# Folding with two stationary matrices, and no subtraction behind the fold

## The chip, the cores and the metric

One core of a Trainium2 chip runs the kernel. The metric is the device time of one execution in microseconds (us), the median of several runs. Below, PE is TensorE, DVE is VectorE, ACT is ScalarE, POOL is GpSimd and SP is SyncE.

## The reference

The input x has 64 batches of 32 rows and 512 columns. Two layers with residuals follow one another:

```python
def layer0(x, W0, condition):              # W0: (16, 32, 32)
    return x + jnp.einsum('bct,bcd->bdt', x, W0[condition])

def layer1(x, label, W, A, Bw):            # W: (512, 512), A: (5, 512, 32), Bw: (512, 32)
    base = jnp.einsum('bsi,oi->bso', x, W)
    low = jnp.einsum('bsi,bir->bsr', x, A[label])
    return x + base + 0.5 * jnp.einsum('bsr,or->bso', low, Bw)
```

The label of a batch is 0, 1 or 2 in the data; the kernel serves the labels 0 to 4.

## The kernel before

**Numbers.** PE multiplies operands of the rounded type float32r. Where a product needs more precision, a float32 value v is split into a rounded part `v_hi`, which ACT writes by a copy to float32r, and a remainder `v_lo`, which DVE writes as v minus `v_hi`. A product is then three matmuls: hi by hi, hi by lo, lo by hi.

**Order of the algebra.** The kernel applies layer 1 first, along the columns, and then layer 0, along the rows within a batch; both are linear. A tile is four batches, 128 rows by 512 columns; there are 16 tiles, worked on in 8 pairs (`pair`), of which pairs 1 to 6 are three turns of a loop with two pairs each (`Fori`). The order on each engine is written out by hand, and semaphores tie the engines together.

**Preparation.** PE transposes W (`transpose_w`, L522) after DVE has added the identity to its diagonal blocks (`add_identity`, L387). The term of label 0 is added to it as a product of two stacks (L556), so that `m_hi` and `m_lo` hold W transposed plus the identity plus what label 0 gives. DVE does all this in one long sequence, with the first two transposes of x in the middle of it. POOL builds `ident` and `fold_id`, a column of four 32 by 32 identities, and gathers the rows of W0 by indirect DMAs (L229), two for each pair.

**A pair.** DVE transposes x (L332), ACT and DVE split it into `xt_hi` and `xt_lo` (L259, L339). On PE:
- `low_pair` (L483 to L485) computes, for the four other labels, x times (A of that label minus A of label 0): 128 rows (label, r) by the 256 rows of the pair, in `p_low`.
- DVE multiplies by a 0/1 mask (`keep_low`, L352), so that each column keeps at most one of the four groups of 32 rows. ACT and DVE split the result: `kept_hi` (L295), `kept_lo` (L359).
- `fold_pair` (L501, L502) sums the four groups with the stationary matrix `fold_r`: four copies of `fold_id` side by side. So the sum stands four times in `p_fold`, in rows 0 to 31, 32 to 63 and so on. `kept_hi` goes through the matrix first, then `kept_lo` is accumulated onto it.
- ACT copies `p_fold` to `low_stack` in float32r (L303). DVE then overwrites the lower half, rows 64 to 127, with `p_fold` minus that rounded value (L444). So `low_stack` holds the rounded part twice, and then the remainder twice. `delta_tile` (L506) multiplies it by `b_stack`, and adds the product to `p_u`, which `main_tile` (L495 to L497) has filled with the product of x and m.
- `mix_tile` (L512 to L515) applies layer 0 to `u_hi` and `u_lo`, the parts of `p_u`, with a block-diagonal matrix `diag_hi` and `diag_lo`. DVE makes it from the gathered W0 (`mix` L448, `diag` L451). ACT copies the result to `y_sb` (L269), and SP stores it (L196).

**Order around the change.** On DVE the pair is: `keep_low`, first transpose, `kept_lo`, second transpose, `xt_lo` of the first tile of the next pair, then the subtraction L444, then `mix`, `diag`, `xt_lo` of the second tile, `diag_lo`, and the two `u_lo`. POOL's next gather waits for `diag` (L246). PE issues `delta_tile` as the last thing in a pair, after the wait for `s_stack` (L575). SP loads x two pairs ahead, but in one queue with the stores: the load of pair p + 3 stands behind the store of pair p (L196 to L202).

```python
            with sp.Fori(0, LOOPS) as g:
                for slot in range(2):
                    sp.wait_ge(s_xt, 2 * (2 * g + slot) + 2)
                    load(2 * g + slot + 2, slot)
                    store(2 * g + slot)
```

Of the kernel before, what the change touches and what calls it, by code (L numbers as in the profile page):

```python
# [27 lines left out]
F32 = mybir.dt.float32  # L28
F32R = mybir.dt.float32r
I32 = mybir.dt.int32  # L30
ALU = mybir.AluOpType
COPY = mybir.ActivationFunctionType.Copy

P = 128


def conditioned_lora_kernel(nc, x, cond, label, W0, W, A, Bw, out):
    B, S, T = x.shape
    NL, _, R = A.shape
    O = W.shape[0]  # L40
    BT = P // S
# [4 lines left out]
    Q = P // R  # L46
    ROWS = 2 * P
# [13 lines left out]
    with ExitStack() as ctx:  # L61
        def sb(name, shape, dt=F32):
            return ctx.enter_context(nc.sbuf_tensor(name, shape, dt))

        def ps(name, shape):
            return ctx.enter_context(nc.psum_tensor(name, shape, F32))

        def sem(name):
            return ctx.enter_context(nc.semaphore(name))
# [1 line left out]

        ident = sb("ident", [P, P])
        fold_id = sb("fold_id", [P, R])
        fold_r = sb("fold_r", [P, Q, R], F32R)
        block = sb("block", [P, BT])
        p_num = sb("p_num", [P, 1])
        group = sb("group", [P, 1])
# [36 lines left out]
        kept_hi = sb("kept_hi", [P, ROWS], F32R)  # L114
        kept_lo = sb("kept_lo", [P, ROWS], F32R)
        low_stack = sb("low_stack", [P, ROWS], F32R)
# [5 lines left out]
        p_fold = ps("p_fold", [P, O])  # L122
# [13 lines left out]
        s_group = sem("s_group")  # L136
# [21 lines left out]
        s_kepthi = sem("s_kepthi")  # L158
        s_keptlo = sem("s_keptlo")
        s_fold = sem("s_fold")  # L160
        s_foldhi = sem("s_foldhi")
        s_stack = sem("s_stack")


# [85 lines left out]
        @blk.scalar  # L250
        def _(act):
            act.dma_start(w_sb[:, 0], W[0:P, :]).then_inc(s_w_in[0], 16)

            act.dma_start(a_sb[:].rearrange("p l c r -> p l (c r)"), A_cols).then_inc(s_a_in, 16)

            def split_x(t, slot, u):

                act.wait_ge(s_xt, t + 1)
                nc.scalar.activation(xt_hi[:, slot, :, P * u:P * (u + 1)], xt[:, u], COPY).then_inc(s_xhi, 1)  # L259

            def split_u(n, u, bank, cols=slice(0, O)):

                act.wait_ge(s_u, n + 1)
                nc.scalar.activation(u_hi[:, u, cols], p_u[bank][:, cols], COPY).then_inc(s_uhi, 1)  # L264

            def copy_y(t, u):

                act.wait_ge(s_y, t + 1)
                nc.scalar.activation(y_sb[:, bass.ds(t, 1)], p_y[u][:].unsqueeze(1), COPY).then_inc(s_y_copied, 1)  # L269


            act.wait_ge(s_bT, 1)
            nc.scalar.activation(b_hi[:], p_y[0][:], COPY).then_inc(s_stack_hi, 1)
            act.wait_ge(s_adiff, 1)
            nc.scalar.activation(ad_hi[:], a_diff[:], COPY).then_inc(s_adhi, 1)
            act.wait_ge(s_aT, 1)
            nc.scalar.activation(a0_hi[:], p_y[1][:], COPY).then_inc(s_stack_hi, 1)
            split_x(0, 0, 0)
            act.wait_ge(s_less_hi, 1)
            nc.scalar.activation(b_stack[:], p_fold[:], COPY).then_inc(s_y_copied, 1)  # L280
            split_x(1, 0, 1)
            act.wait_ge(s_less_hi, 2)
            nc.scalar.activation(a0_stack[:], p_low[:], COPY).then_inc(s_y_copied, 1)

            def split_m(c):

                act.wait_ge(s_m, c + 1)
                nc.scalar.activation(m_hi[:, c], p_u[c][:], COPY).then_inc(s_uhi, 1)

            for c in range(C):  # L290
                split_m(c)

            def pair(p, slot, first=False, last=False):
                act.wait_ge(s_kept, p + 1)
                nc.scalar.activation(kept_hi[:], kept[:], COPY).then_inc(s_kepthi, 1)  # L295
                for u in range(2):
                    if not first:
                        copy_y(2 * p - 2 + u, u)
                    if not last:
                        split_x(2 * p + 2 + u, 1 - slot, u)  # L300
                    if u == 0:
                        act.wait_ge(s_fold, p + 1)
                        nc.scalar.activation(low_stack[:], p_fold[:, 0:ROWS], COPY).then_inc(s_foldhi, 1)  # L303
                act.wait_ge(s_diag32, p + 1)
                nc.scalar.activation(diag_hi[:, slot], diag[:, slot], COPY).then_inc(s_diaghi, 1)
                if not last:
                    split_u(2 * p, 0, 2 * slot)
                    split_u(2 * p + 1, 1, 2 * slot + 1)

            pair(0, 0, first=True)  # L310
            with act.Fori(0, LOOPS) as g:
                for slot in (1, 0):
                    pair(2 * g + 2 - slot, slot)
            pair(PAIRS - 1, 1, last=True)
            split_u(TILES - 2, 1, 3, left)
            split_u(TILES - 1, 0, 2)
            split_u(TILES, 1, 0, right)
            copy_y(TILES - 2, 0)

        @blk.vector  # L320
        def _(dve):
# [13 lines left out]
            def split_x(t, slot, u):  # L335

                dve.wait_ge(s_xhi, t + 1)
                cols = slice(P * u, P * (u + 1))
                nc.vector.tensor_tensor(xt_lo[:, slot, :, cols], xt[:, u], xt_hi[:, slot, :, cols].bitcast(F32),  # L339
                                        ALU.subtract).then_inc(s_xlo, 1)  # L340
# [22 lines left out]
            for j in range(BT):  # L363
                nc.vector.memset(group[R * j:R * (j + 1)], float(j)).then_inc(s_group, 1)
            nc.vector.memset(block[:], 0.0).then_inc(s_group, 1)
            dve.wait_ge(s_group, BT + 1)
            for j in range(BT):
                nc.vector.memset(block[R * j:R * (j + 1), j:j + 1], 1.0).then_inc(s_group, 1)
            dve.wait_ge(s_pool, 1)
# [14 lines left out]
            def add_identity(o):  # L384
                dve.wait_ge(s_w_in[o], 16)
                w_diag = w_sb[:, o, P * o:P * (o + 1)]
                nc.vector.tensor_tensor(w_diag, w_diag, ident[:], ALU.add).then_inc(s_diag, 1)  # L387
# [11 lines left out]
                nc.vector.tensor_scalar(to[:], ident[:], groups[:, 0:1], None, ALU.mult).then_inc(s_negative, 1)  # L399

            dve.wait_ge(s_pool, 4 + Q)
            add_identity(0)
            dve.wait_ge(s_x_in[0], 16 * Q)
            transpose_x(0, 0)
# [3 lines left out]
            split_x(0, 0, 0)  # L408
            add_identity(3)
            split_x(1, 0, 1)  # L410
            nc.vector.tensor_copy(fold_r[:], fold_id[:].unsqueeze(1).broadcast_to([P, Q, R])).then_inc(s_group, 1)
            dve.wait_ge(s_label_in, 16)
            nc.vector.tensor_scalar(keep[:], label_b[:], -1.0, group[:, 0:1], ALU.add,
                                    ALU.is_equal).then_inc(s_group, 1)
# [4 lines left out]
                nc.vector.tensor_tensor(m_lo[:, c], p_u[c][:], m_hi[:, c].bitcast(F32),  # L419
                                        ALU.subtract).then_inc(s_mlo, 1)  # L420

            dve.wait_ge(s_group, 2 * BT + 3)
            for c in range(C - 1):
                split_m(c)
            keep_low(0)
# [4 lines left out]
            def pair(p, slot, used, landed, first=False, last=False):  # L430
# [9 lines left out]
                if not last:  # L440
                    transpose_x(1 - slot, 1)
                    split_x(2 * p + 2, 1 - slot, 0)
                dve.wait_ge(s_foldhi, p + 1)
                nc.vector.tensor_tensor(low_stack[P // 2:P], p_fold[P // 2:P, 0:ROWS],  # L444
                                        low_stack[P // 2:P].bitcast(F32), ALU.subtract).then_inc(s_stack, 1)

                dve.wait_ge(s_w0_in[slot], 32 * used)
                nc.vector.tensor_tensor(mix[:, slot], w0_sel[:, bass.ds(2 * p, 2)],  # L448
                                        fold_id[:].unsqueeze(1).broadcast_to([P, 2, S]), ALU.add).then_inc(s_dve, 1)
# [27 lines left out]
        def _(pe):  # L477
            mm = nc.tensor.matmul
# [19 lines left out]

            def fold_pair():

                mm(p_fold[:, 0:ROWS], fold_r[:], kept_hi[:], start=True, stop=False)  # L501
                mm(p_fold[:, 0:ROWS], fold_r[:], kept_lo[:], start=False, stop=True).then_inc(s_fold, 1)  # L502

            def delta_tile(bank, u, cols=slice(0, O)):

# [112 lines left out]
```

## Time and profile before

| what | value |
|---|---|
| three runs | 94.54, 94.93, 95.05 us, median 94.93 us |
| span of the profiled execution, first to last instruction | 92.8 us |
| median less that span | 2.1 us |
| PE, DVE, ACT, POOL busy | 90%, 68%, 45%, 24% of the span |
| mean granted TensorE clock | 0.982 |
| HBM traffic | 5.96 MB read, 4.19 MB written |

The profiled execution is known by its span alone; what lies around the span in a timed run is taken as the 2.1 us between the two. A timeline row gives the start, the duration and the instruction, and in brackets how long the engine was idle before it and what ended that. The durations of successive instructions on an engine overlap, so the distance from start to start says what an instruction costs its engine. "PEld" is the weight load of PE, which runs beside the matmul before it. Clock 1.00 is 2.4 GHz, clock 0.50 is 1.2 GHz.

### The profile page before, as it was taken

The numbers are of one execution on the slowest core, as the hardware profiler recorded it, in microseconds if no ns is written. First come the engines' busy times: TensorE is split into PE (matmuls) and PEld (weight loads), VectorE is DVE, ScalarE is ACT, GpSimd is POOL, SyncE is SP. The second block draws the span as 40 slices with busy tenths as digits, with TensorE's granted clock in tenths as the row PEclk, the third lists the DMA queues.
The fourth block names the chain that finished last, engine by engine and source line by source line (L and its number), as shares of the span: only waits on it lengthen the run. The fifth ranks groups of instructions, "written<-read, shape, count | busy, mean of one in ns | idle before, by whom it ended". The sixth has DMA issues, their size and how long they took to land.

```text
span 92.8 us, 1445 instructions
## 1 busy us (share of the span) xinstructions
PE 83.6 (90%) x436; PEld 71.3 (77%) x436; DVE 63.1 (68%) x135; ACT 42.1 (45%) x82; POOL 22.1 (24%) x30
## 2 busy tenths in 40 slices
PE   2940979999999999999999999999999999999970
PEld 2930969988888898689878987898789868989950
DVE  2109997899988743994599549854986398624650
ACT  2321355625653643464346435543554355434540
POOL 5205779400620430026003500350044000000000
PEclk9999589999999999999999999999999999999999
DMA  1899985300000293019403920392048204100505
GB/s 14 242 204 214 277 153 161 92 0 0 10 15 0 99 262 106 0 73 286 107 0 119 275 72 0 136 264 67 0 164 242 61 0 161 69 7 0 226 0 226
DMA packets 13460, 10.21 MB, mean 110 GB/s; under 512 B 1808, under 2 KB 10896, under 8 KB 13456
## 3 DMA queue, kind: packets, MB, share of 16 engines
q1 hardware_dynamic: 12144, 9.31, 35.3%
q10 hardware_dynamic: 800, 0.59, 2.4%
q0 software_dynamic: 512, 0.26, 1.4%
q8 instruction: 2, 0.03, 0.2%
q14 instruction: 2, 0.02, 0.1%
HBM read 5.96 MB, written 4.19 MB: 110 GB/s over the span
## 4 chain that ended last, share of the span: by engine, by line
PE 68%; DMA 13%; SPq 5%; issue 5%; DVE 4%; ACT 1%; ACTq 0%
PE p_u L496 12%; PE p_u L495 12%; PE p_u L497 12%; DMA x_sb<-in_x 7%; DMA cond_b<-in_itok_B 6%; PE p_y L515 3%; PE p_y L512 3%; PE p_y L513 3%; PE p_low L483 3%; SPq L185 3%; PE p_low L485 3%; PE p_low L484 3%; PE p_u L506 3%; PE p_u L522 2%; PE p_fold L501 2%
## 5 line engine op out<-in xcount | busy, mean ns | idle before, releaser
L229 POOL DMA_INDIRECT w_sel<-in_L_cond_weights,w_row x16 | 17.8, 1112 | 42.2 <-DVE diag L451 39.2
L496 PE MATMUL p_u<-m_lo,xt_hi 128*128 128x512 f32 (+1 forms) x68 | 25.6, 377 | 0.0
L495 PE MATMUL p_u<-m_hi,xt_hi 128*128 128x512 f32 (+1 forms) x68 | 25.6, 377 | 0.0
L497 PE MATMUL p_u<-m_hi,xt_lo 128*128 128x512 f32 (+1 forms) x68 | 25.6, 377 | 0.0
L332 DVE STREAM_TRANSPOSE xt<-x_sb 128x512 f32<-128x512 f32 x16 | 17.3, 1091 | 6.7 <-DMA x_sb<-in_x 6.6
L345 DVE TENSOR_TENSOR u_lo<-p_u,u_hi 128x512 fp32r<-128x512 f32 (+1 forms) x17 | 10.6, 656 | 8.2 <-ACT u_hi L264 8.1
L259 ACT ACTIVATE xt_hi<-xt 128x512 fp32r<-128x512 f32 x16 | 10.1, 629 | 10.9 <-DVE xt L332 10.9
L495 PEld LDWEIGHTS p_u<-m_hi,xt_hi 128*128 128x128 f32 x68 | 12.8, 188 | 2.4
L497 PEld LDWEIGHTS p_u<-m_hi,xt_lo 128*128 128x128 f32 x68 | 12.8, 188 | 2.4
L496 PEld LDWEIGHTS p_u<-m_lo,xt_hi 128*128 128x128 f32 x68 | 12.8, 188 | 2.4
L264 ACT ACTIVATE u_hi<-p_u 128x512 fp32r<-128x512 f32 (+1 forms) x17 | 8.9, 571 | 7.7 <-PE p_u L506 7.7
L339 DVE TENSOR_TENSOR xt_lo<-xt,xt_hi 128x512 fp32r<-128x512 f32 x16 | 10.7, 669 | 0.4 <-ACT xt_hi L259 0.4
L269 ACT ACTIVATE y_sb<-p_y 128x512 f32 (+1 forms) x15 | 8.9, 591 | 3.0 <-PE p_y L515 3.0
L483 PE MATMUL p_low<-xt_hi,ad_hi 128*128 128x256 f32 x32 | 9.0, 282 | 0.0
L485 PE MATMUL p_low<-xt_hi,ad_lo 128*128 128x256 f32 x32 | 8.9, 279 | 0.0
L484 PE MATMUL p_low<-xt_lo,ad_hi 128*128 128x256 f32 x32 | 8.9, 279 | 0.0
L295 ACT ACTIVATE kept_hi<-kept 128x256 fp32r<-128x256 f32 x8 | 3.4, 420 | 9.5 <-DVE kept L352 8.1
L483 PEld LDWEIGHTS p_low<-xt_hi,ad_hi 128*128 128x128 f32 x32 | 6.0, 187 | 0.7 <-DVE xt_lo L339 0.4
L484 PEld LDWEIGHTS p_low<-xt_lo,ad_hi 128*128 128x128 f32 x32 | 6.0, 188 | 0.3
L512 PE MATMUL p_y<-u_hi,diag_hi 128*128 128x512 f32 (+1 forms) x16 | 6.2, 388 | 0.0
L513 PE MATMUL p_y<-u_hi,diag_lo 128*128 128x512 f32 (+1 forms) x16 | 6.2, 387 | 0.0
L515 PE MATMUL p_y<-u_lo,diag_hi 128*128 128x512 f32 (+1 forms) x16 | 6.1, 384 | 0.0
(77 smaller groups left out, 100.8 us busy)
## 6 DMA issues: line engine op xcount, KB each, us to landing
x_sb<-in_x SPq DMA_DIRECT2D x32, 128.0 KB
out<-y_sb SPq DMA_DIRECT2D x7, 512.0 KB
w_sb<-in_L_cond_W SPq DMA_DIRECT2D x3, 256.0 KB, 6.6
out<-y_sb SPq DMA_DIRECT2D x2, 256.0 KB
a_sb<-in_L_cond_lora_A ACTq DMA_DIRECT2D x1, 320.0 KB, 6.4
w_sb<-in_L_cond_W ACTq DMA_DIRECT2D x1, 256.0 KB, 3.2
w_sel<-in_L_cond_weights,w_row POOLq DMA_INDIRECT x16
bw_sb<-in_L_cond_lora_B_w SPq DMA_DIRECT2D x1, 64.0 KB, 3.4
```

Of the source, the lines that this page charges most:

```text
L229: nc.gpsimd.indirect_dma_start(out=w0_sel[:, t, :], out_offset=None, in_=W0_rows, in_offset=bass.IndirectOffsetOnAxis(ap=w0_row[:, t:t + 1 ...
L259: nc.scalar.activation(xt_hi[:, slot, :, P * u:P * (u + 1)], xt[:, u], COPY).then_inc(s_xhi, 1)
L332: nc.vector.transpose(xt[:, u].rearrange("p c (b s) -> p c b s", s=S), x_sb[:, slot, u].rearrange("p b (i c) -> p c b i", c=C)).then_inc(s ...
L339: nc.vector.tensor_tensor(xt_lo[:, slot, :, cols], xt[:, u], xt_hi[:, slot, :, cols].bitcast(F32), ALU.subtract).then_inc(s_xlo, 1)
L345: nc.vector.tensor_tensor(u_lo[:, u, cols], p_u[bank][:, cols], u_hi[:, u, cols].bitcast(F32), ALU.subtract).then_inc(s_ulo, 1)
L483: mm(p_low[:, 0:ROWS], ad_hi[:, c], xt_hi[:, slot, c], start=(c == 0), stop=False)
L484: mm(p_low[:, 0:ROWS], ad_hi[:, c], xt_lo[:, slot, c], start=False, stop=False)
L485: last = mm(p_low[:, 0:ROWS], ad_lo[:, c], xt_hi[:, slot, c], start=False, stop=(c == C - 1))
L495: mm(to, xt_hi[:, slot, c, rows], m_hi[:, c, cols], start=(c == 0), stop=False)
L496: mm(to, xt_hi[:, slot, c, rows], m_lo[:, c, cols], start=False, stop=False)
L497: mm(to, xt_lo[:, slot, c, rows], m_hi[:, c, cols], start=False, stop=False)
L512: mm(to[:, cols], diag_hi[:, slot, u], u_hi[:, u, cols], start=True, stop=False)
```

## The change

The fold gets two stationary matrices, kept in one tile `fold_to`. The first has `fold_id` in columns 0 to 63 (twice, 32 columns each) and zeros in columns 64 to 127; the second has zeros first and then `fold_id` twice. `kept_hi` goes through the first and `kept_lo` through the second, accumulated in the same bank. So `p_fold` holds the sum of `kept_hi` twice and then the sum of `kept_lo` twice, and ACT's copy (L303) writes the whole of `low_stack`. Its semaphore increment is now that of `s_stack`, for which PE waits. The subtraction L444, its wait and the semaphore `s_foldhi` are gone. For the new tile DVE clears `fold_parts` at its start, copies `fold_id` into two blocks of it before `add_identity(0)`, and casts all of it to `fold_to` where it made `fold_r`.

```diff
--- before.py
+++ after.py
@@ -71,7 +71,8 @@
 
         ident = sb("ident", [P, P])
         fold_id = sb("fold_id", [P, R])
-        fold_r = sb("fold_r", [P, Q, R], F32R)
+        fold_parts = sb("fold_parts", [P, 2, 2, 2, R])
+        fold_to = sb("fold_to", [P, 2, 2, 2, R], F32R)
         block = sb("block", [P, BT])
         p_num = sb("p_num", [P, 1])
         group = sb("group", [P, 1])
@@ -158,7 +159,6 @@
         s_kepthi = sem("s_kepthi")
         s_keptlo = sem("s_keptlo")
         s_fold = sem("s_fold")
-        s_foldhi = sem("s_foldhi")
         s_stack = sem("s_stack")
 
 
@@ -300,7 +300,7 @@
                         split_x(2 * p + 2 + u, 1 - slot, u)
                     if u == 0:
                         act.wait_ge(s_fold, p + 1)
-                        nc.scalar.activation(low_stack[:], p_fold[:, 0:ROWS], COPY).then_inc(s_foldhi, 1)
+                        nc.scalar.activation(low_stack[:], p_fold[:, 0:ROWS], COPY).then_inc(s_stack, 1)
                 act.wait_ge(s_diag32, p + 1)
                 nc.scalar.activation(diag_hi[:, slot], diag[:, slot], COPY).then_inc(s_diaghi, 1)
                 if not last:
@@ -363,7 +363,8 @@
             for j in range(BT):
                 nc.vector.memset(group[R * j:R * (j + 1)], float(j)).then_inc(s_group, 1)
             nc.vector.memset(block[:], 0.0).then_inc(s_group, 1)
-            dve.wait_ge(s_group, BT + 1)
+            nc.vector.memset(fold_parts[:], 0.0).then_inc(s_group, 1)
+            dve.wait_ge(s_group, BT + 2)
             for j in range(BT):
                 nc.vector.memset(block[R * j:R * (j + 1), j:j + 1], 1.0).then_inc(s_group, 1)
             dve.wait_ge(s_pool, 1)
@@ -399,6 +400,9 @@
                 nc.vector.tensor_scalar(to[:], ident[:], groups[:, 0:1], None, ALU.mult).then_inc(s_negative, 1)
 
             dve.wait_ge(s_pool, 4 + Q)
+            for part in range(2):
+                nc.vector.tensor_copy(fold_parts[:, part, part],
+                                      fold_id[:].unsqueeze(1).broadcast_to([P, 2, R])).then_inc(s_group, 1)
             add_identity(0)
             dve.wait_ge(s_x_in[0], 16 * Q)
             transpose_x(0, 0)
@@ -408,7 +412,8 @@
             split_x(0, 0, 0)
             add_identity(3)
             split_x(1, 0, 1)
-            nc.vector.tensor_copy(fold_r[:], fold_id[:].unsqueeze(1).broadcast_to([P, Q, R])).then_inc(s_group, 1)
+            dve.wait_ge(s_group, 2 * BT + 4)
+            nc.vector.tensor_copy(fold_to[:], fold_parts[:]).then_inc(s_group, 1)
             dve.wait_ge(s_label_in, 16)
             nc.vector.tensor_scalar(keep[:], label_b[:], -1.0, group[:, 0:1], ALU.add,
                                     ALU.is_equal).then_inc(s_group, 1)
@@ -419,7 +424,7 @@
                 nc.vector.tensor_tensor(m_lo[:, c], p_u[c][:], m_hi[:, c].bitcast(F32),
                                         ALU.subtract).then_inc(s_mlo, 1)
 
-            dve.wait_ge(s_group, 2 * BT + 3)
+            dve.wait_ge(s_group, 2 * BT + 6)
             for c in range(C - 1):
                 split_m(c)
             keep_low(0)
@@ -440,10 +445,6 @@
                 if not last:
                     transpose_x(1 - slot, 1)
                     split_x(2 * p + 2, 1 - slot, 0)
-                dve.wait_ge(s_foldhi, p + 1)
-                nc.vector.tensor_tensor(low_stack[P // 2:P], p_fold[P // 2:P, 0:ROWS],
-                                        low_stack[P // 2:P].bitcast(F32), ALU.subtract).then_inc(s_stack, 1)
-
                 dve.wait_ge(s_w0_in[slot], 32 * used)
                 nc.vector.tensor_tensor(mix[:, slot], w0_sel[:, bass.ds(2 * p, 2)],
                                         fold_id[:].unsqueeze(1).broadcast_to([P, 2, S]), ALU.add).then_inc(s_dve, 1)
@@ -498,8 +499,8 @@
 
             def fold_pair():
 
-                mm(p_fold[:, 0:ROWS], fold_r[:], kept_hi[:], start=True, stop=False)
-                mm(p_fold[:, 0:ROWS], fold_r[:], kept_lo[:], start=False, stop=True).then_inc(s_fold, 1)
+                mm(p_fold[:, 0:ROWS], fold_to[:, 0], kept_hi[:], start=True, stop=False)
+                mm(p_fold[:, 0:ROWS], fold_to[:, 1], kept_lo[:], start=False, stop=True).then_inc(s_fold, 1)
 
             def delta_tile(bank, u, cols=slice(0, O)):
```

DVE's order in the preparation, before (`w_sb<-w_sb,ident` is `add_identity`, `xt` are the transposes of x):

```order
L399 TENSOR_SCALAR b_negative<-ident,b_lo_groups 128x128
L399 TENSOR_SCALAR a_negative<-ident,a_lo_groups 128x128
L387 TENSOR_TENSOR w_sb<-w_sb,ident 128x128
L332 STREAM_TRANSPOSE xt<-x_sb 128x512 x2
L387 TENSOR_TENSOR w_sb<-w_sb,ident 128x128 x2
L339 TENSOR_TENSOR xt_lo<-xt,xt_hi 128x4x128
L387 TENSOR_TENSOR w_sb<-w_sb,ident 128x128
L339 TENSOR_TENSOR xt_lo<-xt,xt_hi 128x4x128
L411 CAST fold_r<-fold_id 128x128
```

and with the change, where the line numbers from L366 on have moved by one to five:

```order
L400 TENSOR_SCALAR b_negative<-ident,b_lo_groups 128x128
L400 TENSOR_SCALAR a_negative<-ident,a_lo_groups 128x128
L404 COPY fold_parts<-fold_id 128x64 x2
L388 TENSOR_TENSOR w_sb<-w_sb,ident 128x128
L332 STREAM_TRANSPOSE xt<-x_sb 128x512 x2
L388 TENSOR_TENSOR w_sb<-w_sb,ident 128x128 x2
L339 TENSOR_TENSOR xt_lo<-xt,xt_hi 128x4x128
L388 TENSOR_TENSOR w_sb<-w_sb,ident 128x128
L339 TENSOR_TENSOR xt_lo<-xt,xt_hi 128x4x128
L416 CAST fold_to<-fold_parts 128x256
```

Two copies stand now ahead of the first `add_identity`, and with it ahead of all that follows; the cast is 256 columns wide instead of 128. Neither list shows the clearing of `fold_parts`, which is near DVE's start.

DVE's order in the first pair of a loop turn, from `xt_lo` of the first tile of the next pair to its `diag_lo`, before (`mix` and `diag` are layer 0's matrices; ISA and REGISTER_ALU rows are register work and waits):

```order
L339 TENSOR_TENSOR xt_lo<-xt,xt_hi 128x4x128
L444 TENSOR_TENSOR low_stack<-p_fold,low_stack 64x256
L447 ISA
L448 ISA
L448 TENSOR_TENSOR mix<-w_sel,fold_id 128x64
L450 REGISTER_ALU
L451 TENSOR_TENSOR diag<-mix,block 128x256
L337 REGISTER_ALU
L339 TENSOR_TENSOR xt_lo<-xt,xt_hi 128x4x128
L457 TENSOR_TENSOR diag_lo<-diag,diag_hi 128x256
```

and with the change:

```order
L339 TENSOR_TENSOR xt_lo<-xt,xt_hi 128x4x128
L448 ISA
L449 ISA
L449 TENSOR_TENSOR mix<-w_sel,fold_id 128x64
L451 REGISTER_ALU
L452 TENSOR_TENSOR diag<-mix,block 128x256
L337 REGISTER_ALU
L339 TENSOR_TENSOR xt_lo<-xt,xt_hi 128x4x128
L458 TENSOR_TENSOR diag_lo<-diag,diag_hi 128x256
```

The subtraction is gone, and `mix` follows `xt_lo` directly. PE, ACT, POOL and SP issue the same instructions in the same order as before.

## Rows read from the trace of the kernel before

**Rows 1.** The page's part 4: the chain that ended last, shares of the span by engine
```profile
PE 68%; DMA 13%; SPq 5%; issue 5%; DVE 4%; ACT 1%; ACTq 0%
```

**Rows 2.** Stretch of one pair: us; busy PE, PEld, DVE, ACT, POOL; clock; DMA; GB/s
```profile
42.20:51.20 9.00, 9.00 (x47) 7.57 (x47) 6.63 (x12) 4.55 (x9) 2.09 (x3) 1.00 0.40 120
```

**Rows 3.** Waits of all engines: who waited for whom, us in total, times, longest
```profile
DVE xt L332 <- DMA x_sb<-in_x: 6.6, 5, 1.5
...
PEld p_fold L501 <- DVE kept_lo L359: 2.1, 5, 0.6
```

**Rows 4.** The chain of waits around 33 us: start us, us, what
```profile
33.41 3.36 DMA x_sb<-in_x
```

**Rows 5.** Timeline of DVE in the pair from 33 to 42 us, and into the next
```profile
39.82 0.43 DVE L444 TENSOR_TENSOR low_stack<-p_fold,low_stack 64x256 fp32r<-64x256 f32 x1
40.28 0.23 DVE L448 TENSOR_TENSOR mix<-w_sel,fold_id 128x64 f32<-128x64 f32 x1
...
40.88 0.69 DVE L339 TENSOR_TENSOR xt_lo<-xt,xt_hi 128x512 fp32r<-128x512 f32 x1
...
43.08 1.29 DVE L345 TENSOR_TENSOR u_lo<-p_u,u_hi 128x512 fp32r<-128x512 f32 x2 [1.18 <-ACT u_hi L264]
...
45.81 1.09 DVE L332 STREAM_TRANSPOSE xt<-x_sb 128x512 f32<-128x512 f32 x1 [1.10 <-DMA x_sb<-in_x]
```

**Rows 6.** Timeline of ACT in the same pair
```profile
38.78 0.39 ACT L303 ACTIVATE low_stack<-p_fold 128x256 fp32r<-128x256 f32 x1 [0.24 <-PE p_fold L502]
...
40.07 0.62 ACT L259 ACTIVATE xt_hi<-xt 128x512 fp32r<-128x512 f32 x1
```

**Rows 7.** Timeline of PE in the same pair: delta_tile
```profile
42.03 0.61 PE L506 MATMUL p_u<-b_stack,low_stack 128*128 128x512 f32 x2
```

**Rows 8.** Timelines of DVE and of PE in the last pair
```profile
84.76 0.43 DVE L444 TENSOR_TENSOR low_stack<-p_fold,low_stack 64x256 fp32r<-64x256 f32 x1 [2.53 <-ACT low_stack L303]
...
86.27 0.52 PE L506 MATMUL p_u<-b_stack,low_stack 128*128 128x256 f32 x2
```

**Rows 9.** The chain of waits from 9 to 18 us
```profile
13.14 0.60 issue
13.74 1.76 PE p_u L522 x12
```

**Rows 10.** Timeline of DVE in the preparation
```profile
4.23 0.43 DVE L373 TENSOR_SCALAR bw_rep<-bw_sb 128x512 f32<-128x512 f32 x1 [2.25 <-DMA bw_sb<-in_L_cond_lora_B_w]
...
9.69 1.40 DVE L399 TENSOR_SCALAR b_negative<-ident,b_lo_groups 128x128 fp32r<-128x128 f32 x1
11.00 0.28 DVE L399 TENSOR_SCALAR a_negative<-ident,a_lo_groups 128x128 fp32r<-128x128 f32 x1
11.20 0.30 DVE L387 TENSOR_TENSOR w_sb<-w_sb,ident 128x128 f32<-128x128 f32 x1
...
13.45 0.44 DVE L387 TENSOR_TENSOR w_sb<-w_sb,ident 128x128 f32<-128x128 f32 x2
...
15.22 0.21 DVE L411 CAST fold_r<-fold_id 128x128 fp32r<-128x128 f32 x1
15.36 0.24 DVE L413 TENSOR_SCALAR keep<-label_b,group 128x64 f32<-128x64 int32 x1
16.47 1.89 DVE L419 TENSOR_TENSOR m_lo<-p_u,m_hi 128x512 fp32r<-128x512 f32 x3 [0.87 <-ACT m_hi L288]
```

**Rows 11.** Timeline of POOL in the preparation
```profile
9.72 1.27 POOL L241 TENSOR_TENSOR ad_lo<-a_diff,ad_hi 128x512 fp32r<-128x512 f32 x1 [0.81 <-ACT ad_hi L275]
11.17 1.10 POOL L229 DMA_INDIRECT w_sel<-in_L_cond_weights,w_row  x1 [0.17 <-issue]
...
13.83 2.43 POOL L229 DMA_INDIRECT w_sel<-in_L_cond_weights,w_row  x1 [0.30 <-issue]
```

**Rows 12.** Two stretches of the preparation, columns as in rows 2
```profile
9.20:11.60 2.40, 2.35 (x11) 2.35 (x12) 2.12 (x11) 0.97 (x2) 1.70 (x2) 0.50 1.10 271
13.10:13.80 0.70, 0.10 (x2) 0.06 (x1) 0.70 (x3) 0.70 (x3) 0.42 (x1) 1.00 0.49 111
```

## The prediction

> **What bounds the kernel now.** I read the page's chain of waits first, then stretches of the pair loop, then the waits, and then timelines at the places that the diff touches. The chain shows PE in 68% of the span, DMA in 13%, and DVE in only 4% [rows 1]. In the stretch of one pair PE is busy for 9.00 of 9.00 us and DVE for 6.63 us [rows 2]. So in the pairs the matmuls set the pace, and DVE has some 2.4 us of slack in each. What else shows in the pairs is small: the weight load of the fold waits for `kept_lo` five times, 2.1 us in all [rows 3]. The reader should see why `kept_lo` is late. It stands behind a transpose, and that transpose waits for x from DMA, also five times, 6.6 us in all [rows 3]. The load takes 3.36 us in the chain [rows 4], and SP issues it behind a store. No row of waits names the subtraction L444 as something that PE waits for.
>
> **The subtraction goes.** It costs DVE 0.43 us, and `mix` starts 0.46 us after it [rows 5]; over eight pairs DVE loses 8 x 0.46 = 3.7 us of work. What is it worth to PE? In the pair shown it ends at 39.82 + 0.43 = 40.25, and `delta_tile`, which needs it, starts at 42.03 [rows 5, 7], so 1.8 us remain. ACT's copy, which now releases PE, ended at 38.78 + 0.39 = 39.17 [rows 6]; the margin grows to 2.9 us and PE gains nothing. The last pair is the tightest place: the subtraction ends at 84.76 + 0.43 = 85.19, and PE starts its `delta_tile` at 86.27 [rows 8], with 1.1 us in hand. Nothing there either. That ACT, not DVE, now gives `s_stack` adds no wait, since DVE had waited for the same copy.
>
> **What moves up behind it.** `mix` and `diag` start 0.46 us earlier. The `xt_lo` of the second tile would start at 40.42, but its input `xt_hi` ends at 40.07 + 0.62 = 40.69 [rows 6]; before it started at 40.88 [rows 5], so it gains at most 0.2 us. Then comes `u_lo`, before which DVE is idle for 1.18 us until ACT and PE have produced `u_hi` [rows 5]. The gain ends in that idle time, which grows to about 1.4 us. The next `kept` and the transposes stand behind `u_lo` and behind the load of x [rows 5], and neither comes earlier. POOL's gather starts 0.46 us earlier, because it waits for `diag`; nobody waits for the gathered rows. **Worth: 0 us.** The cover is the wait for `u_hi`. If it were gone, the upper end would be those 3.7 us, but PE with 9.00 us of 9.00 [rows 2] has no room to use them. PE can only win its 2.1 us of waiting [rows 3], and these hang on the load.
>
> **The fold itself.** Two matmuls of 128 x 256 stay two matmuls of 128 x 256, each with its own weight load as before. 0 us.
>
> **Clearing `fold_parts`.** 256 columns on DVE near 1.3 us. No row has a clear of this width. From below it is nothing, from above it is the 0.43 us of the 512-wide operation [rows 10]. Behind it DVE is idle for 2.25 us until `Bw` lands [rows 10]. 0 us, and still 0 us at the upper end.
>
> **The wider cast.** The cast of 128 columns delays its successor by 15.36 - 15.22 = 0.14 us [rows 10]. With 256 columns that may become at most twice as much, 0.28 us. Behind it DVE is idle for 0.87 us until ACT has `m_hi` [rows 10]. 0 us.
>
> **The two copies of 128 x 64.** They are the one addition without cover. From 9.69 us on DVE works without a stop, and the second `add_identity` (13.45 us) is what PE waits for: it ends near 13.45 + 0.27 = 13.72, and PE, after 0.60 us of standing, begins the transposes of W at 13.74 [rows 9, 10]. Whatever is put ahead of it moves PE, and from there on the chain is PE's own, or depends on PE through the store ahead of the load. Nothing later absorbs the shift. The price of a copy: the cast over 128 columns costs a step of 0.14 us. The operation over 512 columns takes 0.43 us against its 0.21 us, so 64 columns less save (0.43 - 0.21) / 384 x 64 = 0.04 us [rows 10]. That leaves 0.10 us each, **0.20 us together**. From below: half of the cast's step, 0.07 us each, so 0.14 us. From above: 0.24 us each, the full duration of the operation over 64 columns at 15.36 [rows 10], so 0.48 us. I take 0.20, since the cast is the nearest in kind.
>
> **Sum.** Against the profiled span: 92.8 + 0.2 = 93.0 us. The median of the runs lies 2.1 us above that span, and I leave this as it is: 94.93 + 0.20 = **95.13 us**. With the bounds, 95.07 to 95.41 us. About 0.5%, 0.47 us, is what a measurement of this kernel can tell from no change, so this forecast counts as within it.
>
> **Rival A: the earlier gather frees the load of x (faster).** In the pairs the load and the gather's transfers are under way together, and the first wait for x was longer than that of the next pair (up to 1.5 us, against 1.10 us [rows 3, 5]). If the gather's earlier start took transfers out of the load's way, all five waits could come down to 1.10 us: 6.6 - 5 x 1.10 = 1.1 us. The time would be 95.13 - 1.1 = 94.0 us. For it: PE does wait for this load, through `kept_lo`. Against it: the load lasts over 3 us [rows 4], and 0.46 us does not move the gather out of it. It decides if the load gets shorter than 3.0 us in each pair.
>
> **Rival B: the copies wait for POOL's gather (slower).** POOL starts the first gather at 11.17 us for 1.10 us [rows 11], and the copies would start at 11.20. The row of `b_negative` shows what such a meeting can cost: 1.40 us instead of 0.28 us, beside POOL's subtraction from 9.72 to 10.99 [rows 10, 11]. If the copies are held until the gather ends at 12.27, DVE and PE are late by 12.27 - 11.20 + 0.20 = 1.27 us, which gives 96.2 us. Against it: the cast at 15.22 and the operation at 15.36 ran inside a gather (13.83 to 16.26) and took 0.21 and 0.24 us [rows 10, 11]. That same gather was the longest, 2.43 us, so if one of the two loses it may be POOL, and its rows are used only by `mix` in the pairs. It decides if a copy lasts over 0.5 us.
>
> The Trainium skill speaks for this rival ("SBUF — State Buffer", "SBUF: two separate sides"): VectorE in a two-port mode, which a float32 copy enters, and GpSimd hold a shared port pair one at a time, and the one that starts later is blocked entirely. By it the sum would be Rival B's 1.27 us, not 0.20. The trace agrees for `b_negative` (1.40 us) and not for the cast at 15.22 us (0.21 us).
>
> **Rival C: PE's longer stop costs clock (slower).** After a long wait PE was granted 0.50 in the stretch 9.20 to 11.60; during the stop at 13.1 it kept 1.00 [rows 12]. The stop grows from 0.60 to 0.80 us. If it brought another such stretch, with half of 2.40 us lost: 95.13 + 1.2 = 96.3 us. Little speaks for it, as the clock did not stir at 0.60 us.
>
> **How the numbers follow.** Forecast 0.69, Rival A 0.12, Rival B 0.14, Rival C 0.05. Of the forecast's share 0.02 may fall below 94.46 and 0.02 above 95.40 by the scatter of runs (94.54 to 95.05). So faster by over 0.5% has 0.12 + 0.02 = 0.14, slower 0.14 + 0.05 + 0.02 = 0.21, and within 0.5% is left 0.65. The range takes in the forecast with its bounds and Rival B, and leaves out most of Rival A, and C: 94.3 to 96.2 us. The forecast's own range is 94.9 to 95.4 us.
>
> **What would show it.** In the new profile the two copies should take about 0.15 us each, the second `add_identity` start at 13.65 and PE's stop be about 0.8 us. DVE should be busy for some 3 us less, with `u_lo` idle for 1.4 us before it in the pairs, and PE's distance from pair to pair unchanged near 9.0 us. The forecast is wrong if a copy lasts over 0.5 us (B), if the waits for x fall clearly under 6.6 us (A), if the clock shows a second low stretch (C), or if PE waits for `s_stack` anywhere.

## The result and the profile after

| | before | changed |
|---|---|---|
| median of seven runs | 94.98 us | 97.36 us |
| lowest, highest | 94.54, 95.72 us | 96.32, 97.71 us |
| span of the profiled execution | 92.8 us | 94.5 us |

The ratio is 1.0246 with a 95% interval of [1.0202, 1.0290]: the change makes the kernel **slower by 2.4 us**. The prediction was 95.13 us, with a range that ended at 96.2 us. The ratios in this text leave disturbed runs out; where these are many (20 of the 31 runs of the kernel before in experiments 5 to 7, two of the four in experiment 3), a ratio lies up to 0.8% from that of the two medians beside it.

The profiled execution of the changed kernel is its fastest run, 96.32 us, so the two traces show 1.7 of the 2.4 us, and no trace shows the rest. First the page's busy times and its chain, by engine and by line:

```profile
PE 84.9 (90%) x436; PEld 72.0 (76%) x436; DVE 59.8 (63%) x130; ACT 41.4 (44%) x82; POOL 20.6 (22%) x30
...
PE 38%; DMA 24%; SPq 11%; DVE 10%; issue 10%; ACT 3%; ACTq 0%; DVEq 0%
DMA x_sb<-in_x 19%; SPq L185 7%; PE p_u L496 6%; PE p_u L498 6%; PE p_u L497 6%; DMA cond_b<-in_itok_B 5%; ACT y_sb L269 3%; SPq L196 3%; PE p_y L516 3%; PE p_y L513 3%; PE p_y L514 3%; DVE xt L332 3%; PE p_fold L502 2%; PE p_u L523 2%; DVE kept_lo L359 2%
```

In [rows 1] the chain lay on PE for 68% and on DMA for 13%. Now it is 38% and 24%, and the load of x leads the list by line. DVE is busy for 59.8 us instead of 63.1 us, so the removed work is gone as planned. It bought nothing.

The waits that answer to [rows 3] (us in total, times, longest; L502 is the fold's first matmul, L501 before):

```profile
DVE xt L332 <- DMA x_sb<-in_x: 8.8, 5, 2.1
...
PEld p_fold L502 <- DVE kept_lo L359: 4.4, 5, 1.2
...
PE p_fold L502 <- DVE kept_lo L359: 2.0, 3, 0.8
```

The transposes wait for x for 8.8 us instead of 6.6 us, again five times. The fold's weight load waits for `kept_lo` for 4.4 us instead of 2.1 us. The five loads as they stand in the chain of the changed kernel (start us, us, what):

```profile
32.95 3.83 DMA x_sb<-in_x
...
42.93 3.84 DMA x_sb<-in_x
...
52.84 3.19 DMA x_sb<-in_x
...
62.17 3.65 DMA x_sb<-in_x
...
71.88 3.28 DMA x_sb<-in_x
```

In the chain of the kernel before only two of the five appear, with 3.36 us [rows 4] and 3.26 us. Now all five are on it: PE waits in every one of these pairs. The stretch of one pair, with the columns of [rows 2], shows the hole in PE, 8.21 us busy of 9.00, where [rows 2] had 9.00 of 9.00:

```profile
42.80:51.80 9.00, 8.21 (x43) 6.70 (x42) 6.19 (x11) 4.07 (x9) 0.97 (x2) 1.00 0.33 84
```

**The same pair in both traces.** By chance SP begins to issue the load of one pair at 41.37 us in either trace. First POOL and SP of the kernel before:

```profile
41.24 1.15 POOL L229 DMA_INDIRECT w_sel<-in_L_cond_weights,w_row  x1 [7.85 <-DVE diag L451]
```

```profile
41.37 1.87 SPq L185 DMA_DIRECT2D x_sb<-in_x  x4
```

Then POOL and SP of the changed kernel:

```profile
40.63 0.95 POOL L229 DMA_INDIRECT w_sel<-in_L_cond_weights,w_row  x1 [8.26 <-DVE diag L452]
```

```profile
41.37 2.03 SPq L185 DMA_DIRECT2D x_sb<-in_x  x4
```

And DVE of the changed kernel, which answers to [rows 5]:

```profile
39.68 0.22 DVE L449 TENSOR_TENSOR mix<-w_sel,fold_id 128x64 f32<-128x64 f32 x1
39.94 0.42 DVE L452 TENSOR_TENSOR diag<-mix,block 128x256 f32<-128x256 f32 x1
40.73 0.69 DVE L339 TENSOR_TENSOR xt_lo<-xt,xt_hi 128x512 fp32r<-128x512 f32 x1 [0.37 <-ACT xt_hi L259]
...
43.07 1.29 DVE L345 TENSOR_TENSOR u_lo<-p_u,u_hi 128x512 fp32r<-128x512 f32 x2 [1.32 <-issue]
...
46.79 1.08 DVE L332 STREAM_TRANSPOSE xt<-x_sb 128x512 f32<-128x512 f32 x1 [2.10 <-DMA x_sb<-in_x]
```

The reader should see three things. `mix` follows `xt_lo` without the subtraction and starts at 39.68 (40.28 in [rows 5]). The gather starts at 40.63 instead of 41.24. And x, whose load was issued at the same time, releases the transpose at 46.79 instead of 45.81: **the load releases the transpose 0.98 us later, and of the transfers around it the gather is the one that moved ahead**. In the packet records of the two traces the load's last packet ends at 45.28 and at 45.94 us, so 0.66 us of the 0.98 lie in the packets. SP's four issues also take 0.16 us longer (2.03 against 1.87 us). That this isn't what makes the load late, experiment 4 shows: there two pairs with issues of 1.87 and 1.90 us wait for 1.72 and 1.97 us, where the kernel before, with issues of 1.87 and 1.89 us, waits for 1.10 and 1.22 us.

The sum over the pairs: when SP issues the store in front of the first load that PE waits for, the changed kernel is 0.44 us ahead (30.51 against 30.95 us), because data landed 0.81 us earlier in its preparation. The two chains show it, the kernel before first:

```profile
1.25 5.51 DMA cond_b<-in_itok_B
```

```profile
1.25 4.70 DMA cond_b<-in_itok_B
```

The five waits grow by 8.8 - 6.6 = 2.2 us. 92.8 - 0.44 + 2.2 = 94.6 us, and the span is 94.5 us. So the waits for x account for the whole difference of the two traces. The loop's pace says the same: the transposes that wait for x are (73.43 - 36.80) / 4 = 9.16 us apart before and (75.18 - 36.80) / 4 = 9.60 us after.

### The profile page after: what moved, and what is told of

Same layout as the page of the kernel before. It is cut to its first block, busy times and chain, and to the rows that moved or that the text cites. A ratio compares the mean times of both kernels' runs of the same rounds, so it can differ in the third digit from the quotient of the medians.

```text
span 94.5 us, 1439 instructions
## 1 busy us (share of the span) xinstructions
PE 84.9 (90%) x436; PEld 72.0 (76%) x436; DVE 59.8 (63%) x130; ACT 41.4 (44%) x82; POOL 20.6 (22%) x30
## 4 chain that ended last, share of the span: by engine, by line
PE 38%; DMA 24%; SPq 11%; DVE 10%; issue 10%; ACT 3%; ACTq 0%; DVEq 0%
DMA x_sb<-in_x 19%; SPq L185 7%; PE p_u L496 6%; PE p_u L498 6%; PE p_u L497 6%; DMA cond_b<-in_itok_B 5%; ACT y_sb L269 3%; SPq L196 3%; PE p_y L516 3%; PE p_y L513 3%; PE p_y L514 3%; DVE xt L332 3%; PE p_fold L502 2%; PE p_u L523 2%; DVE kept_lo L359 2%
## 5 line engine op out<-in xcount | busy, mean ns | idle before, releaser
L229 POOL DMA_INDIRECT w_sel<-in_L_cond_weights,w_row x16 | 16.2, 1013 | 45.5 <-DVE diag L452 42.6
```

The costliest lines, as they stand in the source:

```text
L229: nc.gpsimd.indirect_dma_start(out=w0_sel[:, t, :], out_offset=None, in_=W0_rows, in_offset=bass.IndirectOffsetOnAxis(ap=w0_row[:, t:t + 1 ...
```

## The experiments

**The theory (G).** Removing the subtraction brings `diag` forward, and with it POOL's gather. The gather's transfers now reach the DMA engines at the moment when the load of x begins there, and delay it. PE waits for that load, because it is issued late, behind a store. **Rivals.** The new preparation costs the time; the two matrices cost PE time; the new timing on DVE and ACT disturbs the pairs by itself.

**1. The preparation alone.** The kernel before, with `fold_parts` and `fold_to` made and never used:

```diff
+            nc.vector.memset(fold_parts[:], 0.0).then_inc(s_group, 1)
...
+            for part in range(2):
+                nc.vector.tensor_copy(fold_parts[:, part, part],
+                                      fold_id[:].unsqueeze(1).broadcast_to([P, 2, R])).then_inc(s_group, 1)
...
+            dve.wait_ge(s_group, 2 * BT + 4)
+            nc.vector.tensor_copy(fold_to[:], fold_parts[:]).then_inc(s_group, 1)
```

> The kernel before, with only the preparation of the change added: fold_parts is cleared, filled by the two copies and cast to fold_to, and nothing uses it (fold_r is still made and used). Theory G (the earlier gather delays the load of x): no change in the pairs, so 95.0 to 95.3 us, the waits of the transposes for x near 6.6 us. Rival P (the preparation costs the time, by the copies or by where it leaves the engines): near 97.3 us.

Measured: 94.35 us against 94.41 us of the kernel before on that chip, ratio 0.9994 [0.9920, 1.0069]. The five waits for x in its trace are 6.5 us. The preparation isn't the cause. Its own 0.2 us is below what this comparison can tell.

**2. The removal alone.** The matrix stays, the subtraction goes; the lower half of `low_stack` is then not the remainder:

```diff
-                dve.wait_ge(s_foldhi, p + 1)
-                nc.vector.tensor_tensor(low_stack[P // 2:P], p_fold[P // 2:P, 0:ROWS],
-                                        low_stack[P // 2:P].bitcast(F32), ALU.subtract).then_inc(s_stack, 1)
```

> The kernel before, with only the subtraction behind the fold left out (the lower half of low_stack then holds the rounded part instead of the remainder) and the one matrix fold_r kept. Theory G: DVE comes to diag 0.46 us earlier and POOL's gather with it, so the load of x is late as in the changed kernel: 97.0 to 97.5 us, waits for x near 8.8 us. Rival P, and a rival by which the two matrices themselves cost time on PE: 94.9 to 95.1 us.

Measured: 95.88 us against 94.41 us, ratio 1.0175 [1.0094, 1.0255]. Its wait for x:

```profile
DVE xt L332 <- DMA x_sb<-in_x: 8.5, 5, 2.2
```

Leaving work out makes the kernel slower, with 8.5 us of waiting, and without the new matrices. The size is under the 97.0 us expected; the kernel before ran 0.6 us faster on this chip than in the first comparison, which is part of that.

**3. The gather alone, first try.** The kernel before whole; only POOL's wait is another:

```diff
-                    pool.wait_ge(s_diag32, p - 1)
+                    pool.wait_ge(s_dve, p)
```

> The kernel before whole, with one edit on POOL: the gather for a pair waits for mix of two pairs earlier instead of for diag, and so starts some 0.5 us earlier. DVE, ACT and PE do the same work. Theory G: 96.8 to 97.6 us, waits for x near 8.8 us. A rival by which DVE's or ACT's new timing itself delays the pairs: 95.0 us.

Measured: 95.69 us against 94.41 us, ratio 1.0064 [0.9949, 1.0178]. Not enough to tell, and under the forecast. The trace is of its run of 96.01 us, above its median, and shows waits for x of 7.3 us, between the two kernels. In the table below this run's gather does not come as early, measured against the load, as that of the changed kernel.

**4. The gather alone, second try.** The kernel before with the gather released by the end of the subtraction, some 0.25 us earlier again. So that the semaphore of the gathered rows stays in order, DVE's wait for them stands now ahead of the subtraction:

```diff
-                    pool.wait_ge(s_diag32, p - 1)
+                    pool.wait_ge(s_stack, p - 1)
...
+                dve.wait_ge(s_w0_in[slot], 32 * used)
                 dve.wait_ge(s_foldhi, p + 1)
...
-                dve.wait_ge(s_w0_in[slot], 32 * used)
```

> The kernel before, with the gather waiting for the end of the subtraction instead of for diag, some 0.7 us earlier than in the kernel before and 0.2 to 0.3 us earlier than in the run in which it waited for mix (DVE's wait for the gathered rows stands ahead of the subtraction now, where it costs nothing). Theory G: the first gather ends within 0.2 us after SP begins to issue the load of x in every second pair, as in the changed kernel, so waits for x of 8 to 9.5 us and 96.3 to 97.5 us, with all of DVE's, ACT's and PE's work as before. A rival by which the gather alone cannot do it: under 95.7 us.

Measured: 96.82 us against 94.81 us, ratio **1.0217 [1.0177, 1.0257]**. All the work of the kernel before, in the same order on every engine, and nearly the whole loss of the change (1.0246). Waits, and in one pair POOL's gather beside SP's load:

```profile
DVE xt L332 <- DMA x_sb<-in_x: 8.3, 5, 2.0
...
PEld p_fold L501 <- DVE kept_lo L359: 3.9, 5, 1.1
```

```profile
59.34 0.95 POOL L229 DMA_INDIRECT w_sel<-in_L_cond_weights,w_row  x1 [7.40 <-DVE low_stack L445]
```

```profile
60.17 1.90 SPq L185 DMA_DIRECT2D x_sb<-in_x  x4
```

No row of waits shows DVE waiting for the gathered rows, so the moved wait costs nothing. This settles where the time comes from.

**5. The subtraction's time put back.** The changed kernel, with a subtraction of the same size on DVE that writes a tile nobody reads:

```diff
+                dve.wait_ge(s_stack, p + 1)
+                nc.vector.tensor_tensor(spare[P // 2:P], p_fold[P // 2:P, 0:ROWS],
+                                        low_stack[P // 2:P].bitcast(F32), ALU.subtract).then_inc(s_spare, 1)
```

> The changed kernel, with a subtraction of the same size put back on DVE at the old place; it writes a spare tile that nobody reads. PE, the matrices and the values are those of the changed kernel. Theory G: diag and with it the gather move back by 0.46 us, and the time returns to that of the kernel before plus the 0.2 us of the preparation: 94.3 to 95.2 us, waits for x near 6.6 us. A rival by which the matrices cost time on PE: 2 us over the kernel before.

Measured: 94.79 us against 95.12 us, ratio 1.0029 [0.9965, 1.0092]. The waits for x are 6.8 us. Useless work on DVE brings the loss back to nothing. The matrices are cleared too.

**6. The gather later.** In the changed kernel, and then in the kernel before, the gather waits for `diag_lo`:

```diff
-                    pool.wait_ge(s_diag32, p - 1)
+                    pool.wait_ge(s_diaglo, p - 1)
```

> The changed kernel, with one edit on POOL: the gather waits for diag_lo instead of diag, and so starts some 1.3 us later than in the changed kernel, 0.7 us later than in the kernel before. Theory G: its transfers fall in the middle of the load of x or behind it, and the time comes back to 94.5 to 95.3 us, waits for x at or under 6.6 us. The rivals leave it at 97.3 us.

> The kernel before, with the gather waiting for diag_lo instead of diag, some 1.3 us later. Theory G: like the changed kernel with the same edit, 92.3 to 93.2 us on this theory alone, waits for x near 5.6 us.

Measured: the changed kernel 92.72 us against 94.41 us, ratio 0.9838 [0.9756, 0.9919]; the kernel before 94.12 us against 95.12 us, ratio 0.9961 [0.9899, 1.0024]. The wait for x of the changed kernel with this edit:

```profile
DVE xt L332 <- DMA x_sb<-in_x: 5.6, 5, 1.3
```

The waits came out as expected in both, 5.6 and 5.2 us. Both times missed. The changed kernel became faster than both kernels, 1.8 us under the 94.5 to 95.3 us expected, so the direction held and the size did not; the kernel before on that chip was 0.6 us faster than in the first comparison. The kernel before with the edit came out 0.9 us over its 92.3 to 93.2 us.

**7. The gather behind the whole load.** Again in both kernels:

```diff
-                    pool.wait_ge(s_diag32, p - 1)
+                    pool.wait_ge(s_kept, p)
```

> The changed kernel, with the gather for a pair waiting for kept of the pair before (instead of diag of two pairs before), some 4 us later than in the changed kernel: its transfers fall behind the whole load of x. Theory G: the load of x runs alone, waits of the transposes for x at or under the 5.6 us of the run with the gather behind diag_lo, time 92.2 to 93.0 us. If that other run won by something else than the distance to the load: 93.5 us or more.

> The kernel before, with the same edit on POOL. Theory G: the subtraction is worth nothing once the gather is out of the load's way, so the same time as the changed kernel with this edit, less the 0.2 us of its preparation: 92.0 to 92.9 us. If the subtraction's removal has a cost or a gain of its own in the pairs, the two differ by over 0.5 us.

Measured: the changed kernel 93.51 us against 95.12 us, ratio 0.9908 [0.9853, 0.9962]; the kernel before 94.06 us against 95.12 us, ratio 0.9954 [0.9903, 1.0005]. The wait for x in the changed kernel with this edit, and one such transpose:

```profile
DVE xt L332 <- DMA x_sb<-in_x: 4.9, 5, 1.0
...
PEld p_fold L502 <- issue: 0.2, 1, 0.2
```

```profile
44.70 1.09 DVE L332 STREAM_TRANSPOSE xt<-x_sb 128x512 f32<-128x512 f32 x1 [0.96 <-DMA x_sb<-in_x]
```

The waits are 4.9 us, and 4.7 us in the kernel before with this edit, the shortest of all. The weight load of the fold waits for 0.2 us, and no longer for `kept_lo`. So the pairs run at PE's own pace, (71.56 - 35.84) / 4 = 8.93 us. Both medians lie above the forecasts, by 0.5 and 1.2 us. The traces were of the fastest runs (92.73 and 92.54 us), and can't show what made the others slower; that stays open. The two ratios overlap, so whether the removal is worth anything once the gather is away stays open here.

**The dose.** For the last four pairs with a wait for x, from the traces: how long after SP begins to issue the load (SP L185) POOL ends the first of its two gathers (L229, start plus duration), and how long the transposes then wait in these four pairs together.

| kernel | first gather ends after the load's issue begins, us | waits for x, four pairs, us |
|---|---|---|
| before, gather with the subtraction (4) | 0.1 to 0.4 | 6.99 |
| changed | 0.2 to 0.5 | 6.84 |
| before, subtraction left out (2) | 0.2 to 0.5 | 7.34 |
| before, gather behind `mix` (3) | 0.4 to 0.7 | 5.47 |
| before | 1.0 to 1.3 | 5.03 |
| before, with the preparation (1) | 1.0 to 1.3 | 4.90 |
| changed, with the useless subtraction (5) | 1.0 to 1.3 | 5.13 |
| changed, gather behind `diag_lo` (6) | 1.6 to 1.9 | 4.36 |
| before, gather behind `diag_lo` (6) | 1.7 to 2.0 | 4.14 |
| changed, gather behind `kept` (7) | 4.5 to 4.8 | 3.83 |
| before, gather behind `kept` (7) | 4.5 to 4.8 | 3.76 |

The later the gather, the shorter the waits, up to the scatter: two kernels with the same distances differ by up to 0.5 us in the sum, and single pairs by some 0.3 us. The largest step lies between a gather that ends 0.2 to 0.5 us after and one that ends 0.4 to 0.7 us after. Kernels with and without the subtraction lie on one curve. The kernel before stood on its slope: with 5.03 us against 3.76 us it paid for the gather too, only less. The first of the five pairs isn't counted here: in some of these kernels its first gather ends before the load's issue begins, and its wait doesn't follow the order of the table (1.34 us with the gather with the subtraction, 1.53 us before, 1.98 us changed).

**8. The load of x ahead of the store.** If the gather hurts only because PE waits for the load, an earlier load must make it harmless:

```diff
+            sp.wait_ge(s_xt, 2)
+            load(2, 0)
-            with sp.Fori(0, LOOPS) as g:
+            with sp.Fori(0, LOOPS - 1) as g:
                 for slot in range(2):
-                    sp.wait_ge(s_xt, 2 * (2 * g + slot) + 2)
-                    load(2 * g + slot + 2, slot)
+                    sp.wait_ge(s_xt, 2 * (2 * g + slot) + 4)
+                    load(2 * g + slot + 3, 1 - slot)
                     store(2 * g + slot)
+            sp.wait_ge(s_xt, 2 * (PAIRS - 4) + 4)
+            load(PAIRS - 1, 1)
+            store(PAIRS - 4)
+            store(PAIRS - 3)
```

> The changed kernel, with one edit on SP: the load of x for pair p + 3 is issued ahead of the store of pair p, not behind it; the gather still waits for diag. Theory G says that the early gather costs time only because PE waits for the load of x that stands behind the store. With the load ahead it has several us in hand: waits of the transposes for x near 0 in the pairs, none of kept_lo, PE near 8.9 us a pair as in the run with the gather behind kept, so 92.5 to 93.9 us although the gather is as early as in the changed kernel. If the early gather disturbs something else too: 95 us or more.

> The kernel before, with the same edit on SP. Theory G: the same pace in the pairs, and without the 0.2 us of the new preparation: 92.3 to 93.9 us, within 0.5 us of the changed kernel with this edit. If the removed subtraction is worth something once the load is out of the way, the changed kernel with this edit is faster by over 0.5 us.

> The changed kernel, with both edits: the load ahead of the store, and the gather behind diag_lo. Theory G: no gain over the load ahead of the store alone, as neither is waited for then: within 0.4 us of it.

Measured, against 94.97 us of the kernel before: changed 93.68 us, ratio 0.9877 [0.9818, 0.9936]; before 93.56 us, ratio 0.9865 [0.9799, 0.9931]; changed with the late gather 92.76 us, ratio 0.9793 [0.9710, 0.9876]. Two stretches of the first, columns as in [rows 2], and one of its transposes:

```profile
36.00:45.00 9.00, 9.00 (x48) 7.72 (x47) 6.23 (x12) 4.49 (x10) 1.89 (x2) 1.00 0.39 121
45.00:54.00 9.00, 9.00 (x48) 7.72 (x47) 6.23 (x12) 4.50 (x10) 1.89 (x2) 1.00 0.40 120
```

```profile
43.83 1.09 DVE L338 STREAM_TRANSPOSE xt<-x_sb 128x512 f32<-128x512 f32 x1
```

PE is busy without a gap, and the transpose waits for nothing: no row of waits names x any more, though the gather still waits only for `diag`. With the load out of danger the two kernels are equal as far as these runs can tell, 93.68 and 93.56 us, each known to some 0.6 us: **no gain and no cost of the removed subtraction itself is to be seen**. The third run missed its forecast by 0.5 us on the fast side. Its pairs run at the same pace, and its trace is shorter in the preparation alone: the fold of the second pair starts at 26.61 us instead of 28.64 us. The intervals of the two overlap, so a gain of the late gather on top isn't shown.

## Why the prediction was wrong

**What bounds the kernel: right, and half used.** PE sets the pace, and the fold's waits come from the load of x behind a store. The prediction named this chain and then treated its 2.1 us only as something to win. Nothing held it at 2.1 us.

**The subtraction on PE's path: right.** No wait for `s_stack` shows in the trace after, and with the load out of danger no worth of the removal is to be seen.

**What moves up behind it: this is the step that failed.** It read: "POOL's gather starts 0.46 us earlier, because it waits for `diag`; nobody waits for the gathered rows. **Worth: 0 us.**" Each half is true (41.24 to 40.63 in the pair shown, 0.61 us), and the conclusion is not. Nobody waits for the rows, but the transfers use the engines of the load that PE waits for. What the runs put in the place of these 0 us is **+2.2 us** of waits for x in the traces, and the gather moved alone gives a ratio of 1.0217. With it fell the sign that the distance from pair to pair stays near 9.0 us: it became 9.60 us.

**Rival A had the place and the wrong sign.** It let an earlier gather only free the load, and dismissed the rest with "0.46 us does not move the gather out of it". That was the very warning: a gather in the middle of a load (before) is cheaper than one at its start. The four pairs of the table went from 5.03 to 6.84 us, where Rival A expected less. A rival with the other sign, at the price of the longest wait in the trace in every pair (1.5 us five times, 7.5 us instead of 6.6 us), would have given +0.9 us, and still less than half.

**The preparation: right.** Timelines of DVE and of POOL after, which answer to [rows 10] and [rows 11]:

```profile
1.34 0.27 DVE L366 MEMSET fold_parts<- 128x256 f32 x1
...
10.19 0.27 DVE L400 TENSOR_SCALAR a_negative<-ident,a_lo_groups 128x128 fp32r<-128x128 f32 x1
10.38 0.30 DVE L404 COPY fold_parts<-fold_id 128x64 f32<-128x64 f32 x2
10.60 0.28 DVE L388 TENSOR_TENSOR w_sb<-w_sb,ident 128x128 f32<-128x128 f32 x1
...
12.83 0.50 DVE L388 TENSOR_TENSOR w_sb<-w_sb,ident 128x128 f32<-128x128 f32 x2
...
14.66 0.28 DVE L416 CAST fold_to<-fold_parts 128x256 fp32r<-128x256 f32 x1
14.87 0.24 DVE L418 TENSOR_SCALAR keep<-label_b,group 128x64 f32<-128x64 int32 x1
16.25 1.89 DVE L424 TENSOR_TENSOR m_lo<-p_u,m_hi 128x512 fp32r<-128x512 f32 x3 [1.14 <-ACT m_hi L288]
```

```profile
10.35 1.10 POOL L229 DMA_INDIRECT w_sel<-in_L_cond_weights,w_row  x1 [0.17 <-issue]
```

The two copies move the next instruction by 10.60 - 10.38 = 0.22 us, against 0.20 us predicted. The clearing (0.27 us) and the wider cast (a step of 0.21 us) lie in idle time. The second `add_identity` starts at 12.83 us and not at the 13.65 us foretold, because of the data that landed 0.81 us earlier. **Rival B** fell: the copies started 0.03 us after the gather and took 0.30 us together, beside a gather that ran until 11.45. The Trainium skill's rule of the shared port pair ("SBUF — State Buffer", "SBUF: two separate sides") does not show here for a gather's instruction. Beside POOL's subtraction, from 8.92 to 10.19 us, `b_negative` again took long, 1.38 us from 8.88 us on. So one of the two is held, as the Trainium skill's rule says. But by the rows it is the one that started 0.04 us earlier, where that rule gives the ports to the one that starts first. In the kernel before the rows have the same order (9.69 and 9.72 us), so the agreement that the prediction saw is only in part one. **Rival C** isn't the cause either. The granted clock of the changed kernel's trace is 1.0, and its three runs at 1.0 took 96.32, 97.13 and 97.36 us, 96.94 us in the mean. The other four had a mean clock of 0.964, under the 0.982 of the kernel before's trace, and took 97.40 us in the mean. So a longer low stretch did come in some runs, and may have cost 0.5 us there. The kernel before has such runs too: of its 31 in experiments 5 to 7, seven were near 0.962, with 95.35 us in the mean against 95.30 us of the eleven at 0.994 or more.

## What to carry to other kernels

When an edit lets a DMA start earlier, ask not only who waits for its data but which transfer it will meet on the DMA engines, and whether anyone waits for that one. A wait in the trace that hangs on a transfer is a price that can grow, so give it both signs. Where the critical load stands in a queue behind a store, move the load ahead first (here -1.3%): then no wait for it was left, though the gather came early.

## What the runs showed of the hardware

**Few packets, a long delay.** Two gathers of 16 KB, each 16 packets of 1 KB beside 16 of 4 bytes, delayed a load of 512 KB by up to 1 us, though the data packets of one gather are 1.6% as many as the load's 1024.

**Which comes first.** In the pair compared above the load's first packet came 1.37 us after SP's first issue before, and 1.75 us after it in the changed kernel, behind the first packets of the gather. Over the four pairs of the table, in the changed kernel, the gather's first packet came ahead of the load's in two (1.46 and 1.48 us after SP's first issue, against 1.75 and 1.70 us), and these pairs waited for 2.10 and 1.91 us, against 1.10 and 1.22 us in the kernel before. In the other two it came behind (2.20 and 2.12 us against 1.70 us), and they waited for 1.37 and 1.46 us, against 1.27 and 1.44 us. So nearly all of the 1.81 us between the two sums lies in the pairs in which the gather came first. It isn't the whole rule: in experiment 4 a pair with the gather behind (2.15 against 1.71 us) still waited for 1.72 us.

**Slow packets.** Counted in the packet records of the traces from 28 us on, 3 of the gathers' 160 packets of 1 KB took over 0.3 us in the kernel before, with 0.45 us the longest. In the changed kernel it was 20 of 160, and the longest took 1.12 us. With the gather behind the whole load it was 2 of 177. But this count doesn't follow the loss: it was 11 of 160 in experiment 4, which lost nearly as much as the change, and 13 of 160 in experiment 3, which lost less. Why a gather's packet takes that long just when a load begins, and how it holds up the load, was not tried, and stays open.
